# Attention in a fused eight-layer kernel: the two score passes change places inside each half step

## The reference, cut to what matters

```python
scores = jnp.einsum('bqhd,bkhd->bhqk', q, k) * scale
scores = scores + bias[None, :, None, :]
scores = jnp.where(causal[None, None, :, :], scores, -1000000000.0)
p = jax.nn.softmax(scores, axis=-1)
ctx = jnp.einsum('bhqk,bkhd->bqhd', p, v).reshape(B, S, D)
return ctx @ Wout.T + b_out
```

## Time and profile before

| | us |
|---|---|
| median of 3 runs | 1620.43 (1616.7 to 1627.98) |
| profiled execution | 1619.1 |
| its span, first to last instruction | 1617.3 |
| loop of attn0 | from about 40 to 302 |
| loop of attn1 | from about 880 to 1165 |

### The profile page before, as it was taken

One profiled execution on the slowest core, in us unless ns is written; L12 is line 12 of the kernel. 1 busy time (PEld: TensorE's weight loads), 2 busy tenths in 40 slices (PEclk: granted clock), 3 DMA queues, 4 the chain that ended last, 5 costly groups with the idle time before them and its releaser, 6 DMA issues. The chain is left out here.

```text
span 1617.3 us, 20802 instructions
## 1 busy us (share of the span) xinstructions
PE 1384.7 (86%) x7632; PEld 970.3 (60%) x7632; DVE 1073.8 (66%) x2187; ACT 623.9 (39%) x1159; POOL 346.3 (21%) x301
## 2 busy tenths in 40 slices
PE   3889999588999678899966899999779889889897
PEld 2545554267888567788852334333258667677676
DVE  5656555387678448767738566667266568898775
ACT  1354444353333224333321555556642334333321
POOL 3311100162433102243331340400040201020010
PEclk9799999789999898999986999999989989999899
DMA  6715320220000000000004413210000000000000
GB/s 144 97 29 73 52 30 2 81 71 1 1 1 1 1 1 1 1 1 1 0 34 49 89 32 58 30 21 2 1 1 1 1 0 1 1 0 1 14 13 26
DMA packets 32173, 39.03 MB, mean 24 GB/s; under 512 B 5986, under 2 KB 27210, under 8 KB 31946
## 3 DMA queue, kind: packets, MB, share of 16 engines
q1 hardware_dynamic: 32074, 37.73, 13.1%
HBM read 14.45 MB, written 2.10 MB: 10 GB/s over the span
## 5 line engine op out<-in xcount | busy, mean ns | idle before, releaser
L1302 DVE TENSOR_REDUCE attn_negm<-ps 128x2 f32<-128x1024 f32 (+3 forms) x256 | 255.9, 1021 | 88.6 <-PE ps L916 46.2
L1127 ACT ACTIVATE attn_probs<-ps 128x512 f32<-128x512 f32 (+3 forms) x512 | 237.1, 515 | 177.6 <-PE ps L944 100.0
L480 POOL TENSOR_TENSOR moe_h_low<-moe_h,moe_h_high 128x512 fp32r<-128x512 f32 x96 | 137.0, 1430 | 316.5 <-ACT moe_h_high L430 316.5
L936 PE MATMUL ps<-attn_qs,attn_ks 99*128 99x512 bf16 (+4 forms) x512 | 153.6, 347 | 30.7 <-ACT attn_probs L1127 18.9
L916 PE MATMUL ps<-attn_ks,attn_qs 96*128 96x512 bf16 (+4 forms) x512 | 142.4, 362 | 31.0 <-DMA attn_ks<-attn_part 20.9
L447 ACT ACTIVATE moe_silu<-ps 128x512 f32<-128x512 f32 x96 | 57.5, 599 | 235.1 <-PE ps L353 234.9
L1685 PE MATMUL ps<-sb_f_down,tail_h 128*128 128x256 f32 x512 | 123.2, 386 | 7.1 <-DVEq L1978 7.1
L936 PEld LDWEIGHTS ps<-attn_qs,attn_ks 102*128 102x128 bf16 (+1 forms) x512 | 49.1, 97 | 126.9 <-ACT attn_probs L1127 100.5
L957 PE MATMUL ps<-attn_probs,attn_va 128*32 128x512 f32 (+3 forms) x1024 | 118.3, 535 | 0.0
L1685 PEld LDWEIGHTS ps<-sb_f_down,tail_h 128*128 128x128 f32 x512 | 98.2, 193 | 24.2 <-DVEq L1978 7.3
L1951 DVE TENSOR_TENSOR tail_h<-tail_silu,ps 128x512 f32<-128x512 f32 x64 | 43.6, 682 | 89.5 <-PE ps L1675 57.3
(11 more groups left out here) (324 smaller groups left out, 3302.4 us busy)
## 6 DMA issues: line engine op xcount, KB each, us to landing
attn_qs<-attn_part SPq DMA_DIRECT2D x96, 128.0 KB, 4.4
attn_ks<-attn_part SPq DMA_DIRECT2D x48, 128.0 KB, 6.2
out_x<-x SPq DMA_DIRECT2D x4, 512.0 KB, 2.7
x<-in_x SPq DMA_DIRECT2D x1, 1536.0 KB, 9.7
attn_ks<-attn_part SPq DMA_DIRECT2D x24, 64.0 KB, 4.6
moe_raw<-in_f_gate SPq DMA_DIRECT2D x2, 512.0 KB, 6.8
moe_raw<-in_f_up SPq DMA_DIRECT2D x2, 512.0 KB, 8.0
moe_raw<-in_f_down SPq DMA_DIRECT2D x2, 512.0 KB, 8.6
```

The lines of the kernel that those rows point to most:

```text
L480: pool.tensor_tensor(hc.low[:, j % RING, :], h[:, j % RING, :], hc.high[:, j % RING, :], ALU.subtract).then_inc(low_done, 1)
L936: last = pe.matmul(ps[:, SC + k, 0:width2(kt)], ks[0:ROWS2, b % 2, hd % KH, kt * P:(kt + 1) * P], qs[0:ROWS2, b % 2, hd, T - width2(kt):T] ...
L1127: act.activation(pr[:, s2 % RING, j, 0:n], ps[:, SC + k, 0:n], ACT.Exp, scale=HD ** -0.5).then_inc(exp_done, 1)
L1302: dve.tensor_reduce(m, ps[:, 2 * half:2 * half + 2, 0:width1(qt)], AX, ALU.max, negate=True).then_inc(r1_free, 1)
```

## The change

In each half step `scores2` and its masks now come ahead of `scores1` and its masks, and each pair of masks comes right behind its scores. No instruction is added or removed, and no other engine's program changes. In attn1, which has no masks, only the two score pairs change places.

```diff
                 for half in range(2):
+                    if 0 <= s2 < STEPS:
+                        scores2(2 * s2 + half)
+                        if causal:
+                            masks2()
                     if s1 < STEPS:
                         scores1(2 * s1 + half)
-                    if 0 <= s2 < STEPS:
-                        scores2(2 * s2 + half)
-                    if causal and s1 < STEPS:
-                        masks1(2 * s1 + half)
-                    if causal and 0 <= s2 < STEPS:
-                        masks2()
+                        if causal:
+                            masks1(2 * s1 + half)
                     if half == 0:
                         for job in middle:
                             do(job)
```

## The result

| | before | after |
|---|---|---|
| median, taken in turn on one chip | 1624.62 us (1615.02 to 1633.64, 22 runs) | 1614.34 us (1606.24 to 1623.92, 22 runs) |
| profiled execution | 1619.1 us | 1616.48 us |
| its span | 1617.3 us | 1614.7 us |
| attn0, context of step 8 to context of step 64 | 213.64 us | 205.75 us |
| attn0, one unit without jobs (contexts 44 to 48) | 12.90 us | 12.02 us |

The ratio is 0.9939, with a 95% interval of 0.9919 to 0.9959: the change takes 9.9 us off (3.3 either way), inside the 1% that was called no change, and clear of zero. A second timing of the same code gave 0.998 (0.9958 to 1.0002). Over all comparisons of this study, whatever the chip, the kernel before has a mean of 1623.2 us (89 runs) and the change 1615.5 us (34 runs), a difference of 7.8 us, some 2 either way. The forecast was -4.7 us.

The account below looks back on a forecast made before the run. Time was taken to be winnable only where PE idles, in the loop of mutual waits between PE and ACT. attn0's -8.3 and attn1's +3.6 gave -4.7 us, a median of 1615.7 us, with 80% from 1607 to 1623.

Parts of the forecast that it names:

- The unit and step 47: attn0 without jobs: contexts 44 to 48 from 12.90 to 12.0 us; step 47's start to second exponentials from 3.11 to 2.45.
- Quarters 1 and 2: attn0: half 0's first-pass masks now run during the exponentials, 0.11 us gained a step; 1.1 and 0.8 in all.
- step 3 into 0: attn0, quarter 3 into quarter 0: a 512-column pair and two mask pairs leave ACT's path, 0.66 us gained.
- The sum for attn0: All attn0 gains less the loss after `merge`: 8.3 us gained, bounds 4 and 12.5.
- The loss of 0.3 behind `merge` at 49 and 57: attn0: ACT's copy holds the exponentials while the 384-column pair now stands behind them; 0.3 us each, 0.6 lost.
- ACT's wait: attn0, sign of being right: ACT's wait for `masks2` down by some 8 us or more.
- The masks stall behind their scores: Rival, attn0: masks adding to a just-written bank cost 0.11 us a pair; time 1618, no separate chance given.
- The first pass turns critical in attn1: Rival, attn1: the first-pass pair before the context costs 0.44 us a step where ACT is late; up to 1637, chance 0.08.
- attn1's term: attn1: plain steps win nothing, steps with an ACT copy lose; 3.6 us lost in all, bounds 0 and 6.6.
- The context copy: attn1: a context copy on ACT, formerly hidden, now costs 0.15 us in six quarters 3; 0.9 lost.
- The flat 0.3 for the other jobs: attn1: other end jobs with an ACT copy (`merge`, `rows`, swapped projection) cost 0.3 us each, nine times; 2.7 lost.
- every later layer simply shifts: Layers behind the attention loops: they only move in time; any that does not was a sign of being wrong.

## Why the prediction was right, and where not

Held against its own steps, one by one:

- **The unit and step 47.** 12.0 and 2.45 us were predicted; 12.02 and 2.44 were measured. Quarters 1 and 2 won 0.11 each, and step 3 into 0 won 0.66 in all, as worked out. Each price, taken as a start-to-start distance from the earlier trace rows, carried over.
- **The sum for attn0.** 8.3 us predicted, 7.9 measured between contexts 8 and 64. Steps 19 and 35 won 0.45 (0.44 said), steps behind `out` 0.11. The loss of 0.3 behind `merge` at 49 and 57 was half that: from 3.03 to 3.18. That the sum came out so near is in part luck. It counted steps 15 and 31 among the plain ones, with 0.66 each, though `rows` stands at their end, and they won 0.04. In its favour, the projections at steps 17, 21, 33 and 37 did not take the gain away, as the sum had them do: 0.09 to 0.10 each.
- **ACT's wait.** Some 8 us less or more was said; it was 16.5, a part of which only changed its name (above).
- **The masks stall behind their scores** (rival). No: exponentials still begin 0.32 after the mask pair.
- **The first pass turns critical in attn1** (rival, slower). Its mechanism is there, but only behind end jobs with a copy on ACT, and plain steps were 3.38 as worked out from the earlier trace rows.
- **attn1's term was mis-sized.** 3.6 us predicted, 2.4 measured in the steps. The context copy was 0.13 to 0.14 against 0.15, five times and not six: step 64 has no first pass to lose. The flat 0.3 for the other jobs was right on average. `merge` and the first `rows` cost 0.21, the second `rows`, which stands with a context copy, and the swapped projections 0.43, together 2.6 against 2.7. What was missing is the 0.43 that steps 17 and 33 each gave back.
- **That every later layer simply shifts was the step that failed** (a layer that does not was among the signs of being wrong), and nothing in the sum had a place for it. The way out of attn0 took back 2.7 to 3.8 us, at a lower granted clock. In attn1 falls of the clock that cost the old order 1.6 to 3.2 us were absent, so the loop, contexts 11 to 64, was 228.5 and 228.6 us against 227.6 and 229.7. On average attn1 cost nothing: 228.5 in the three profiles with the new order throughout, 229.1 in the six with the old.
- **A slip in the bounds.** 0.88 in each of 14 units is 12.3, not 12.5. Nothing hangs on it.

By the traces the whole is then -7.9 in attn0's loop, some +3.4 behind it and 0 to -0.5 in attn1, between -4 and -5 us as far as these stretches go. The forecast of -4.7 has that size, but by luck in its second half, where two terms stand in for each other: it had 3.6 lost in attn1 and none behind attn0. The timings say -7.8, some 2 either way. The some 3 us between stay open. They are no more than single executions can differ by: the two profiled ones of the kernel before lay 4.7 and 1.3 us below the means of their runs, and of those of the change one lay 2.6 above and one 1.0 below. Over the 22 runs of the change the time follows the mean granted clock (correlation -0.85, some 10 us for 0.01). A higher clock isn't what the change won by, though. Its mean was 0.937 in both sets of runs of the change, and 0.937 to 0.938 in the three sets of the kernel before for which it is on record.

## What to carry to other kernels

Where two engines hand single buffers to and fro, find in the timeline the moment when one releases the other, and price what the issuing order puts between that release and the next: it is paid in full. The same work a place later is free as long as there is slack: it was in attn0's plain steps, and in attn1 it came back in front of the context, where nothing was won. Change order in whole pairs, products with the masks that complete them, since the scores alone exchanged cost 6 us and with their masks brought 8. The slack that is left belongs to work from another step: with the context product in the wait for the first exponentials the kernel took 1592.7 us, three to four times the gain of the change.

## What the runs showed of the hardware

- **The granted clock can fall right behind a stretch of full work.** In attn1 of the kernel before, PE was busy for 6.03 us of a step of 6.03, and the next step had a mean clock of 0.75. The same full step in the kernel after was followed by 1.00. Six of six profiles with the old order throughout attn1 had a fall in that step or behind it, none of three with the order of the change, at places that changed from one profile to the next (steps 26, 42 or both).
- **Loops of the same work, issued in another order, leave another clock behind.** After the loop of attn0, 300 to 310 us, the granted clock was 1.00 in both profiles of the kernel before and 0.50 and 0.55 in those of the change. Eight 256-column products took 3.75 in place of 1.97 us. They did so in all seven profiles that ended the loop with `scores2` first, one of a slower loop (219.1 us) among them, and in none of the other five.
- **Step lengths repeat, run times don't.** The loop of attn0, 213.6 us, came out equal to 0.01 us in two profiles of the kernel before. Between contexts 11 and 64 of attn1 the same two differed by 2.1 us, 1.6 of it in the four steps of the table above and 0.5 in step 12, in all of which the granted clock differed.
